# Expert gate and up products from high and low halves, in a one-core transformer layer with attention and a mixture of experts

## Chip, cores and metric

One core of a Trainium2 chip runs the whole layer in one launch. The metric is the device time of that launch in microseconds (us), as the median of several executions; lower is better. Durations of single instructions come from one profiled execution.

## The reference

The input is B, N, HID = 4, 512, 256 in float32, so 2048 tokens. The layer has two halves, each followed by a residual and a layer norm:

```python
x = layernorm(x + attention(x)); x = layernorm(x + ffn(x))
# attention: H = 16 query heads, KV = 4 key heads, D = 128
q, k, v = x @ Wq, x @ Wk, x @ Wv
y   = softmax(causal(rope(q) @ rope(k).T / sqrt(D))) @ v
S_t = S_(t-1) * exp(log_sigmoid(k_t) / 16) + softmax(k)_t v_t^T;  o_t = softmax(q)_t @ S_t
attention = (0.5 * y + 0.5 * o) @ Wo
# ffn: E = 8 experts, F = 176, each token takes its 2 likeliest
p = softmax(x @ gate_w.T); w, e = top_k(p, 2)
ffn = sum over the 2 experts e: w * ((silu(x @ w_gate[e]) * (x @ w_up[e])) @ w_down[e])
```

## The kernel before

**Engines.** Each engine has an instruction stream written out by hand: PE (TensorE), ACT (ScalarE), DVE (VectorE), POOL (GpSimd), SP (which issues DMAs). Instructions of a stream run in order, and the streams meet at semaphores (`wait_ge`, `then_inc`). Nothing reorders them.

**Attention part.** The work is 16 groups g (4 batches by 4 key heads) of C = 4 chunks c of 128 tokens, 64 steps. `step(g, c)` exists once for each engine. PE's order in a step is score, gla_matrix, gate_sums, project (of the chunk two ahead), output (the product with Wo of the step before), turn_weights (transposes of the softmax weights), turn (transposes of the next chunk's queries and decayed features `qd`, then of keys at L523, which waits for this step's add_output), gather (the products with V). The products of projection, scores and output use high and low halves: each f32 operand is split into two f32r tiles, hi (a copy on ACT) and lo (the difference, on POOL or DVE), and hi x hi, hi x lo, lo x hi are summed. POOL's order in a step is weigh_features, move_v, decay (L1500 is its second half; it gives `qd`), rotate, then x_split, split of a staged weight, norm1 and send. DVE adds the output product to the token rows `acc` in add_output (L1064), near the middle of its step.

**Routing.** In the last eight groups, counted as steps k = 0 to 31, the first three batches (set 0, 12 tiles of 128 tokens) are routed beside attention. Tables give the step of each piece and whether DVE does it in the middle ("mid") of its step, before add_output, or at the end ("late"): COMPARE_AT, RANK_AT, EXP_AT, COUNT_AT, BASES_AT, SLOTS_AT. Then `send(t)` (L1566) on POOL writes each token's row twice, by indirect DMA, into the slots of its two experts in DRAM (`slot_x`), two DMAs for a tile, by SEND_AT. Before that SP has cleared the slots. GU_IN and DN_IN give the steps in which SP loads expert weights over the projection weights of key heads that are done.

**Expert loop.** The slots of set 0 make NT_A = 31 tiles, those of the fourth batch (set 1) NT_B = 15; NT = 46. For q = 1 to 47 PE does turn_x(q+1) (L677), gate_up(q) (L689), down(q-2) (L706), turn_h(q-1). ACT does h_out(q-2), x_out(q+1), silu(q) (L908), y_out(q-2) (L917), and its norm2 of finished tokens in q = 42 and 43 and behind the loop. DVE does multiply(q) (L1336) and way_back(q). `gate_up` waits for x_out's copy. In the first iterations DVE and PE also route set 1, and in iterations 14 to 17 POOL sends its four tiles. POOL's `send_back(q)` (L1573) writes a finished tile's rows by indirect DMA into `plane`, from one of YO = 5 buffers `yo`. SP loads slots three tiles ahead (L417), and from q = 38 rows of `plane`, which DVE combines from iteration 37 on (combine, moments2 or shift2 in turn). moments2 and shift2 of a batch use four columns `mv`, `ve`, `rstd`, `nmr` that all batches share, so moments2 waits for norm2 of the batch before.

**The end.** After y_out(45) the last write goes out, SP loads the rows of the last four tiles, DVE combines them, POOL's rs2 gives 1/deviation, ACT normalises, SP stores.

Of the kernel before, what the change touches and what calls it, by code (L numbers as in the profile page):

```python
# [84 lines left out]
def layer_kernel(nc, x_rows, x_cols, wqkv, wo_in, wgu, wdn, gate, rope_cos, rope_sin, cmat, cmask, slot_x, plane, out):  # L85
    with ExitStack() as ctx:
# [10 lines left out]
        with nc.sbuf_tensor("w_hi", [P128, KV * KT2 * QKV], F32R) as w_hi, \  # L97
                nc.sbuf_tensor("w_lo", [P128, KV * KT2 * QKV], F32R) as w_lo:
            pass
        gu_w = sb("gu_w", [P128, E, GUW], F32)  # L100
        spare = sb("spare", [P128, KV * KT2 * QKV - E * GUW], F32)
        dn_w = sb("dn_w", [P128, E, DNW], F32)
        spare2 = sb("spare2", [P128, KV * KT2 * QKV - E * DNW], F32)
        wo_hi = sb("wo_hi", [P128, H * HID], F32R)
        wo_lo = sb("wo_lo", [P128, H * HID], F32R)
# [60 lines left out]
        mv = [None] + [sb(f"mv{i}", [P128, 4, 2], F32) for i in (1, 2)]  # L166
        ve = [None] + [sb(f"ve{i}", [P128, 4], F32) for i in (1, 2)]
        rstd = [None] + [sb(f"rstd{i}", [P128, 4], F32) for i in (1, 2)]
# [27 lines left out]
        nmr = sb("nmr", [P128, TPB], F32)  # L196
# [9 lines left out]
        xT = rqT[:, :].rearrange("p (a n) -> p a n", a=2)  # L206
# [50 lines left out]
        s_zf, s_guw, s_dnw = (sem(n) for n in ("s_zf", "s_guw", "s_dnw"))  # L257
# [5 lines left out]
        s_mark, s_back, s_bf = sem("s_mark"), sem("s_back"), sem("s_bf")  # L263
        s_yg = [sem(f"s_yg{i}") for i in range(4)]
# [10 lines left out]
        wo_jobs = [(wo_in[:, a:b], wo_hi[:, a:b], wo_lo[:, a:b]) for a, b in  # L275
                   ((a, min(a + WJOB, H * HID)) for a in range(H * HID // 2, H * HID, WJOB))]
        jobs = proj_jobs(1) + proj_jobs(2) + wo_jobs[0:2] + proj_jobs(3) + wo_jobs[2:]
        n_attn = len(jobs)

        def jobs_of(g, c):  # L280

            u = C * g + c
            return () if u == 1 else (0, 1) if u == 0 else (u,) if u < n_attn else ()
# [7 lines left out]
        COMPARE_AT = {("late", 9): 0, ("late", 13): 1, ("mid", 21): 2}  # L291
# [3 lines left out]
        SLOTS_AT = {("mid", 24): 0, ("mid", 25): 1}  # L295
        SEND_AT = {25: (0, 2), 26: (2, 4), 27: (4, 6), 28: (6, 8), 29: (8, 10), 30: (10, 12)}
# [9 lines left out]
        GU_IN = {18: (0, 2), 22: (2, 4), 26: (4, 6), 30: (6, 8)}  # L306
        DN_IN = {18: (0, 3), 22: (3, 6), 26: (6, 8)}
# [55 lines left out]
        def _(sp):  # L363
# [31 lines left out]
            def load_experts(k):  # L395
                for e in range(*GU_IN.get(k, (0, 0))):
                    sp.wait_ge(s_proj, C * (NG - KV + last_kv(e, GUW) + 1))
                    sp.dma_start(gu_w[:, e, :], wgu[:, e, :]).then_inc(s_guw, 16)
                for e in range(*DN_IN.get(k, (0, 0))):
                    sp.wait_ge(s_proj, C * (NG - KV + last_kv(e, DNW) + 1))  # L400
                    sp.dma_start(dn_w[:, e, :], wdn[:, e, :]).then_inc(s_dnw, 16)
# [40 lines left out]
            for t in range(NT - 38, TILES):  # L442
                load_rows(t)
            ov = out.rearrange("b (t p) n -> p (b t) n", p=P128)
            for n in range(3):
                sp.wait_ge(s_xo, TPB * (n + 1))
                sp.dma_start(ov[:, TPB * n:TPB * (n + 1), :], acc[:, TPB * n:TPB * (n + 1), BODY]).then_inc(s_out, 16)
# [1232 lines left out]
```

## Time and profile before

| | |
|---|---|
| median of 3 runs | 981.12 us (980.0 to 983.92) |
| the profiled execution | 980.99 us |
| its span, first instruction to last | 979.2 us |
| busy: PE, DVE, ACT, POOL | 928.0, 654.4, 661.8, 636.1 us |
| TensorE's granted clock, mean | 0.98 of full |

A busy time says how long an engine had an instruction running; a wait in brackets behind a row says how long the engine stood before it, and what released it. The granted clock is given as a share of 2.4 GHz, 0.50 is 1.2 GHz.

### The profile page before, as it was taken

How to read it: one execution, taken by the hardware profiler on the slowest of the kernel's cores; microseconds unless marked ns; L12 is line 12 of the kernel's file. 1: busy time of each engine (PE TensorE's matmuls, PEld its weight loads, DVE VectorE, ACT ScalarE, POOL GpSimd, SP SyncE). 2: the span in 40 equal slices, each digit the busy share in tenths (PEclk: the TensorE clock that was granted, in tenths of full speed). 3: DMA queues.
4: the chain of work that ended last, by engine and by line, in shares of the span. 5: the costliest groups of instructions: out<-in, count | busy, mean ns of one | idle time of the engine just before them, and what ended most of it. 6: DMA issues, size and time to landing. Idle time of an engine off the chain costs nothing.

```text
span 979.2 us, 18417 instructions
## 1 busy us (share of the span) xinstructions
PE 928.0 (95%) x5347; PEld 718.5 (73%) x5347; DVE 654.4 (67%) x1597; ACT 661.8 (68%) x2139; POOL 636.1 (65%) x609
## 2 busy tenths in 40 slices
PE   7899999999999999999999999999999989989990
PEld 4678777778787878787887877878777766766770
DVE  4777776767676767677676869676887664431274
ACT  6677777777777777777677776777667664543453
POOL 6878675767565657676767667766658881553342
PEclk9999999999999999999999999999999999997995
DMA  7101100000000000900000000010102121332364
GB/s 250 34 17 33 39 1 2 6 12 6 1 0 0 0 1 10 257 6 2 1 1 1 1 7 6 24 39 3 61 1 79 38 85 45 92 107 84 98 180 133
DMA packets 34050, 43.20 MB, mean 44 GB/s; under 512 B 3756, under 2 KB 27950, under 8 KB 33840
## 3 DMA queue, kind: packets, MB, share of 16 engines
q1 hardware_dynamic: 30224, 33.76, 11.8%
q0 software_dynamic: 3744, 8.43, 2.4%
q8 instruction: 41, 0.67, 0.3%
q14 instruction: 41, 0.34, 0.1%
HBM read 25.58 MB, written 18.43 MB: 45 GB/s over the span
## 4 chain that ended last, share of the span: by engine, by line
PE 85%; DVE 4%; ACT 4%; issue 3%; POOL 2%; another core or an unknown queue 1%; DMA 0%; POOLq 0%; DVEq 0%; ACTq 0%
PE OA L590 14%; PE PR L473 12%; PE S L543 11%; PE MS L563 9%; PE S L572 7%; PE S L689 5%; PE OA L552 5%; PE OA L583 4%; PE OA L706 4%; PE PR L519 3%; PE PR L513 3%; PE S L534 1%; PE MS L502 1%; ACT eqk L821 1%; PE MS L594 1%
## 5 line engine op out<-in xcount | busy, mean ns | idle before, releaser
L1496 POOL TENSOR_TENSOR qd<-eqk,eg 128x512 f32<-128x512 f32 x63 | 75.9, 1205 | 163.1 <-issue 157.2
L590 PE MATMUL OA<-wT,V 128*128 128x512 f32 x320 | 150.2, 600 | 0.2 <-DVE wT L1081 0.2
L783 ACT ACTIVATE S<-S,nm 128x128 f32<-128x128 f32 (+3 forms) x256 | 126.8, 495 | 26.8 <-DVE nm L998 22.8
L821 ACT ACTIVATE eqk<-qkv,nmx 128x128 f32<-128x128 f32 x320 | 124.4, 396 | 6.0 <-DVE nmx L1073 5.5
L998 DVE TENSOR_REDUCE nm<-S 128x2 f32<-128x256 f32 (+3 forms) x128 | 102.0, 817 | 29.1 <-PE S L543 23.4
L590 PEld LDWEIGHTS OA<-wT,V 128*128 128x128 f32 x320 | 60.2, 192 | 70.9 <-issue 70.4
L1484 POOL TENSOR_TENSOR eqk<-eqk,rse 128x640 f32<-128x640 f32 x63 | 79.7, 1265 | 49.9 <-DVE rse L1116 25.7
L1032 DVE TENSOR_TENSOR pr<-S,rl 128x256 f32<-128x256 f32 (+3 forms) x128 | 105.5, 824 | 5.0
L1473 POOL TENSOR_TENSOR rp<-qkv,cos 128x640 f32<-128x640 f32 x64 | 99.9, 1560 | 6.4 <-ACT qkv L811 4.9
L1476 POOL TENSOR_TENSOR rp<-rp,rt 128x640 f32<-128x640 f32 x64 | 99.5, 1554 | 5.0
L1473 POOL TENSOR_TENSOR rt<-qkv,sin 128x640 f32<-128x640 f32 x64 | 99.5, 1555 | 0.0
L842 ACT COPY wT<-S 128x512 f32<-128x512 f32 x96 | 51.6, 591 | 51.7 <-PE S L572 51.7
L1573 POOL DMA_INDIRECT plane<-eqk,back x46 | 45.5, 989 | 61.7 <-ACT eqk L917 52.9
L572 PE MATMUL S<-cm,pr 128*128 128x128 f32 x640 | 80.4, 273 | 3.5 <-DVE pr L1032 3.5
L563 PE MATMUL MS<-wo_hi,oT_hi 128*128 128x256 f32 (+1 forms) x256 | 76.0, 297 | 3.5 <-DVE gc L1041 2.9
L473 PE MATMUL PR<-w_hi,ring_hi 128*128 128x512 f32 (+1 forms) x252 | 74.7, 377 | 1.0 <-ACT qkv L811 1.0
L572 PEld LDWEIGHTS S<-cm,pr 128*128 128x128 f32 x640 | 71.2, 141 | 4.3 <-DVE pr L1032 2.7
L563 PE MATMUL MS<-wo_hi,oT_lo 128*128 128x256 f32 (+1 forms) x256 | 72.2, 282 | 0.0
L563 PE MATMUL MS<-wo_lo,oT_hi 128*128 128x256 f32 (+1 forms) x256 | 72.1, 282 | 0.0
L473 PE MATMUL PR<-w_hi,ring_lo 128*128 128x512 f32 (+1 forms) x252 | 71.1, 363 | 0.0
L543 PE MATMUL S<-KT_hi,rq_hi 128*128 128x256 f32 (+2 forms) x192 | 68.8, 359 | 0.0
L552 PE MATMUL OA<-qdT,kdT 128*128 128x512 f32 x128 | 65.6, 594 | 1.5 <-DVE oT_lo L990 1.5
(173 smaller groups left out, 2506.1 us busy)
## 6 DMA issues: line engine op xcount, KB each, us to landing
qkv<-slot_x SPq DMA_DIRECT2D x46, 129.0 KB
pr<-plane SPq DMA_DIRECT2D x16, 256.0 KB, 3.1
gu_w<-in_wgu SPq DMA_DIRECT2D x8, 352.0 KB, 3.6
slot_x<-zero SPq DMA_DIRECT2D x2, 1290.0 KB, 9.8
stage<-in_wqkv SPq DMA_DIRECT2D x6, 384.0 KB, 3.4
xraw<-in_x_cols SPq DMA_DIRECT2D x16, 128.0 KB, 2.4
acc<-in_x_rows SPq DMA_DIRECT2D x1, 2048.0 KB, 11.1
dn_w<-in_wdn SPq DMA_DIRECT2D x8, 256.0 KB, 4.2
```

The lines of the kernel that those rows point to most:

```text
L473: last = pe.matmul(PR[:, a:b], x[:, cc, k, :], wq_cols(w, kv, k, a, b), start=(i == 0), stop=(i == len(steps) - 1))
L543: last = pe.matmul(S[:, h, 0:n], q[:, h * 128:(h + 1) * 128], k[:, 0:n], start=False, stop=(i == len(steps) - 1), skip_group_check=True)
L552: pe.matmul(OA[:, :], kdT[:, :], qdT[:, c % 2, :], start=True, stop=True).then_inc(s_at, 1)
L563: last = pe.matmul(MS[:, 0:HID], o[:, h * 128:(h + 1) * 128], r, start=(i == 0), stop=(i == len(steps) - 1))
L572: last = pe.transpose(S[:, j, h * 128:(h + 1) * 128], pr[:, h, j * 128:(j + 1) * 128], ident)
L590: last = pe.matmul(OA[:, :], V[:, j, :], wT[:, j, :], start=(c == 0 and j == 0), stop=(j == c))
L783: nc.scalar.activation(S[:, h, 0:n], S[:, h, 0:n], ACT.Exp, bias=nm[:, h:h + 1], scale=1.0, accum_out=ls[:, h:h + 1]).then_inc(s_exp, 1)
L821: last = nc.scalar.activation(eqk[:, par, h * 128:(h + 1) * 128], qkv[:, c % C, h * 128:(h + 1) * 128], ACT.Exp, bias=nmx[:, h:h + 1], sca ...
L998: nc.vector.tensor_reduce(nm[:, 2 * pair:2 * pair + 2], S[:, 2 * pair:2 * pair + 2, 0:n], AX_X, ALU.max, negate=True).then_inc(s_nm, 1)
L1032: nc.vector.tensor_tensor(pr[:, h, 0:n], S[:, h, 0:n], rl[:, h].rearrange("p (h o) -> p h o", o=1) .to_broadcast([P128, 2, n]), ALU.mult). ...
L1473: nc.gpsimd.tensor_tensor(to.rearrange("p (h w d) -> p h w d", w=2, d=64), src, tab, ALU.mult).then_inc(s_rt, 1)
L1476: nc.gpsimd.tensor_tensor(rp[:, c % 2, :], rp[:, c % 2, :], rt[:, :], ALU.add).then_inc(s_rp, 1)
```

## The change

- The expert weights of gate and up are kept as `gu_hi` and `gu_lo` (f32r). They pass through `stage` like the attention weights: SP loads (GU_IN, four steps or fewer ahead), ACT copies the high half at the head of its step, POOL subtracts at the end of its step (SPLIT_AT). `dn_w` comes in one DMA in step 26, over the Wo halves of key heads that are done; `wo` therefore holds both halves, interleaved by key head, and its jobs are 512 columns wide.
- `gate_up` is six f32r products instead of two of f32. x_out writes `xT_hi`, and a new DVE instruction `x_low` writes `xT_lo`; it stands first in DVE's iteration.
- POOL does norm1 and send ahead of split. SEND_AT leaves step 28 out and puts three tiles in step 30 and one in step 31. In the expert loop the eight row writes of set 1 go one in each of the iterations 15 to 22, where two went in each of 14 to 17.
- compare(2) goes from the middle of step 21 to the end of 20, slots from the middle of 24 and 25 to the ends of 23 and 24, and tile_experts(0) from slot_bases (step 23) to the end of 26.
- `mv`, `ve`, `rstd`, `nmr` of the second norm have a column for each of the 16 tiles, and moments2's wait for `s_xo` is gone. combine starts one iteration sooner; norm2 goes one tile in each iteration from q = 40. The last tile is normalised on DVE and stored alone.

The diff, cut to its core:

```diff
-        gu_w = sb("gu_w", [P128, E, GUW], F32)
+        gu_hi = sb("gu_hi", [P128, E, GUW], F32R)
...
+        gu_lo = sb("gu_lo", [P128, E, GUW], F32R)
...
-        wo_hi = sb("wo_hi", [P128, H * HID], F32R)
-        wo_lo = sb("wo_lo", [P128, H * HID], F32R)
...
-        mv = [None] + [sb(f"mv{i}", [P128, 4, 2], F32) for i in (1, 2)]
+        mv = [None] + [sb(f"mv{i}", [P128, (0, 4, TILES)[i], 2], F32) for i in (1, 2)]
...
-        nmr = sb("nmr", [P128, TPB], F32)
+        nmr = sb("nmr", [P128, TILES], F32)
...
-        xT = rqT[:, :].rearrange("p (a n) -> p a n", a=2)
+        xT_hi = rq_hi[:, :].rearrange("p (a n) -> p a n", a=2)
+        xT_lo = rq_lo[:, :].rearrange("p (a n) -> p a n", a=2)
...
+        jobs += [(wgu[:, e, :], gu_hi[:, e, :], gu_lo[:, e, :]) for e in range(E)]
+        SPLIT_AT = {18: 0, 19: 1, 22: 2, 23: 3, 26: 4, 27: 5, 30: 6, 31: 7}
...
-        COMPARE_AT = {("late", 9): 0, ("late", 13): 1, ("mid", 21): 2}
+        COMPARE_AT = {("late", 9): 0, ("late", 13): 1, ("late", 20): 2}
...
-        SLOTS_AT = {("mid", 24): 0, ("mid", 25): 1}
-        SEND_AT = {25: (0, 2), 26: (2, 4), 27: (4, 6), 28: (6, 8), 29: (8, 10), 30: (10, 12)}
+        SLOTS_AT, EXPERTS_AT = {("late", 23): 0, ("late", 24): 1}, ("late", 26)
+        SEND_AT = {25: (0, 2), 26: (2, 4), 27: (4, 6), 29: (6, 8), 30: (8, 11), 31: (11, 12)}
...
-        GU_IN = {18: (0, 2), 22: (2, 4), 26: (4, 6), 30: (6, 8)}
-        DN_IN = {18: (0, 3), 22: (3, 6), 26: (6, 8)}
+        GU_IN = {16: (0, 2), 20: (2, 4), 24: (4, 6), 28: (6, 8)}
+        DN_IN = 26
...
-                if q >= 38:
-                    load_rows(q - 38)
+                if q >= 37:
+                    load_rows(q - 37)
...
-            for t in range(3 * TPB, TILES, 2):
-                sp.wait_ge(s_xo, t + 2)
-                sp.dma_start(ov[:, t:t + 2, :], acc[:, t:t + 2, BODY]).then_inc(s_out, 16)
-            sp.wait_ge(s_out, 16 * 5)
+            for a, b in ((TPB, 2 * TPB), (2 * TPB, 3 * TPB), (3 * TPB, 3 * TPB + 2), (3 * TPB + 2, TILES - 1)):
+                sp.wait_ge(s_xo, b)
+                store(a, b)
+            sp.wait_ge(s_last, 1)
+            store(TILES - 1, TILES)
+            sp.wait_ge(s_out, 16 * 6)
...
-                pe.wait_ge(s_xT, q + 1)
-                for k in range(KT2):
-                    last = pe.matmul(S[:, q % 2, 0:2 * F], xT[:, q % 2, k * 128:(k + 1) * 128],
-                                     expert_cols(gu_w, expert[q], k * 2 * F, (k + 1) * 2 * F), start=(k == 0), stop=(k == KT2 - 1))
+                pe.wait_ge(s_xl, q + 1)
+                steps = [(k, x, w) for k in range(KT2) for x, w in ((xT_hi, gu_hi), (xT_hi, gu_lo), (xT_lo, gu_hi))]
+                for i, (k, x, w) in enumerate(steps):
+                    last = pe.matmul(S[:, q % 2, 0:2 * F], x[:, q % 2, k * 128:(k + 1) * 128],
+                                     expert_cols(w, expert[q], k * 2 * F, (k + 1) * 2 * F), start=(i == 0), stop=(i == len(steps) - 1))
...
-                if q in (42, 43):
-                    for i in ((0, 1) if q % 4 == 2 else (2, 3)):
-                        norm2(0, i)
+                if q >= 40:
+                    norm2(q - 40)
...
+                if not n1:
+                    x_low(0)
+                    x_low(1)
                 add_gla(g, c)
...
+            def x_low(q):
+                dve.wait_ge(s_xT, q + 1)
+                nc.vector.tensor_tensor(xT_lo[:, q % 2, :], PR[:, (q % 2) * 512:(q % 2) * 512 + 256],
+                                        xT_hi[:, q % 2, :].bitcast(F32), ALU.subtract).then_inc(s_xl, 1)
...
-                later(dve, s_xo, TPB * n - 2 + 2 * h)
...
-            later_tiles = {37 + t: t for t in range(3 * TPB)}
+            later_tiles = {36 + t: t for t in range(3 * TPB)}
             for q in range(1, NT + 2):
+                if q + 1 < NT:
+                    x_low(q + 1)
...
+            nc.vector.tensor_scalar(a, a, mv[2][:, TILES - 1, 0:1], rstd[2][:, TILES - 1:TILES], ALU.subtract, ALU.mult).then_inc(s_last, 1)
...
-                if isinstance(g, int):
-                    for j in jobs_of(g, c):
-                        split(j)
                 if k in STATS_AT:
                     norm1(STATS_AT[k])
                 if k in SEND_AT:
                     for t in range(*SEND_AT[k]):
-                        send(t)
+                        for r in range(2):
+                            send(t, r)
+                if isinstance(g, int):
+                    for j in jobs_of(g, c):
+                        split(j)
...
-            sends = {14: 12, 15: 13, 16: 14, 17: 15}
-            deviations = {36 + 2 * i: (i // 2, i % 2) for i in range(5)}
+            sends = {15 + i: (3 * TPB + i // 2, i % 2) for i in range(2 * TPB)}
+            deviations = {35 + 2 * i: (i // 2, i % 2) for i in range(5)}
```

## Rows read from the trace of the kernel before

**Rows 1.** The page, part 1: engine, busy us, share of the span, instructions.

```profile
PE 928.0 (95%) x5347; PEld 718.5 (73%) x5347; DVE 654.4 (67%) x1597; ACT 661.8 (68%) x2139; POOL 636.1 (65%) x609
```

**Rows 2.** Timeline, 874 to 897: start, us, engine, line, operation, [wait before it <-releaser].

```profile
875.19 1.35 PE L689 MATMUL S<-gu_w,rqT 128*128 x4
...
886.75 0.32 ACT L908 ACTIVATE qd<-S 128x176 f32<-128x176 f32 x1 [3.84 <-remote]
...
891.67 2.55 PE L689 MATMUL S<-gu_w,rqT 128*128 x4
...
895.67 1.35 PE L689 MATMUL S<-gu_w,rqT 128*128 x4
```

**Rows 3.** Timeline of one undisturbed tile's TensorE work.

```profile
940.42 1.35 PE L689 MATMUL S<-gu_w,rqT 128*128 x4
...
941.60 1.03 PE L706 MATMUL OA<-dn_w,am 128*128 x4
...
942.90 1.35 PE L689 MATMUL S<-gu_w,rqT 128*128 x4
```

**Rows 4.** Windows: length, busy us (x count) of five engines, clock, DMA share, GB/s.

```profile
792.30:795.70 3.40, 3.40 (x7) 1.32 (x6) 1.47 (x5) 3.31 (x14) 3.32 (x3) 0.50 0.00 0
881.10:894.70 13.60, 11.02 (x26) 7.47 (x27) 1.33 (x7) 3.89 (x12) 5.82 (x6) 0.50 0.27 91
```

**Rows 5.** Timeline of POOL, row writes of set 1: the first and the last of eight.

```profile
872.40 0.97 POOL L1566 DMA_INDIRECT slot_x<-acc,sloti  x1 [0.30 <-issue]
...
885.14 0.96 POOL L1566 DMA_INDIRECT slot_x<-acc,sloti  x1 [0.30 <-issue]
```

**Rows 6.** Timeline of PE, the first three of an output product's 12 matmuls.

```profile
712.62 0.37 PE L563 MATMUL MS<-wo_hi,oT_hi 128*128 128x256 f32 x1
712.82 0.28 PE L563 MATMUL MS<-wo_lo,oT_hi 128*128 128x256 f32 x1
712.94 0.28 PE L563 MATMUL MS<-wo_hi,oT_lo 128*128 128x256 f32 x1
```

**Rows 7.** Groups by line and shape: out<-in, xcount, busy us, mean ns, idle before.

```profile
L1108 DVE TENSOR_TENSOR rq_lo<-PR,rq_hi 128x512 fp32r<-128x512 f32 x48 | 32.6, 679 | 0.0
...
L1524 POOL TENSOR_TENSOR w_lo<-stage,w_hi 128x768 fp32r<-128x768 f32 x6 | 10.9, 1833 | 0.0
```

**Rows 8.** Timeline of DVE: two multiplies of neighbouring tiles, moments2 between.

```profile
939.67 0.34 DVE L1336 TENSOR_TENSOR rp<-qd,S 128x176 f32<-128x176 f32 x1 [0.39 <-ACT qd L908]
...
942.15 0.34 DVE L1336 TENSOR_TENSOR rp<-qd,S 128x176 f32<-128x176 f32 x1
```

**Rows 9.** Timeline, end of the expert loop: y_out and send_back of tile 45.

```profile
957.16 0.37 ACT L917 COPY eqk<-OA 128x256 f32<-128x256 f32 x1 [1.30 <-PE OA L706]
...
960.23 1.04 POOL L1573 DMA_INDIRECT plane<-eqk,back  x1 [0.19 <-issue]
```

**Rows 10.** Timeline around decay of steps 28 and 29.

```profile
778.32 0.45 POOL L1500 TENSOR_TENSOR qd<-eqk,eg 128x128 f32<-128x128 f32 x1
...
779.42 0.60 PE L519 MATMUL PR<-cm,qd 128*128 128x128 f32 x4
...
791.58 0.66 PE L519 MATMUL PR<-cm,qd 128*128 128x128 f32 x4 [2.08 <-POOL qd L1500]
```

**Rows 11.** Timeline, step 31: last row write of set 0, first slots, turn_x, turn_weights.

```profile
808.38 0.96 POOL L1566 DMA_INDIRECT slot_x<-acc,sloti  x1 [0.30 <-issue]
...
812.18 1.75 SPq L417 DMA_DIRECT2D qkv<-slot_x  x4
...
815.15 0.60 PE L677 MATMUL PR<-cm,qkv 128*128 128x128 f32 x4
...
817.60 0.66 PE L572 MATMUL S<-cm,pr 128*128 128x128 f32 x4 [1.85 <-DVE pr L1032]
```

**Rows 12.** Timeline of PE, turn's key transpose behind a late add_output, steps 21 and 25.

```profile
688.93 0.30 PE L523 MATMUL MS<-cm,rp 128*128 128x128 f32 x1 [1.73 <-DVE acc L1064]
...
740.93 0.30 PE L523 MATMUL MS<-cm,rp 128*128 128x128 f32 x1 [1.18 <-DVE acc L1064]
```

More of the change, by code:

```diff
@@ L396, in load_experts @@
                 for e in range(*GU_IN.get(k, (0, 0))):
[L397 to L401, printed above, removed]
+                    load_job(n_attn + e)
+                if k == DN_IN:
+                    sp.wait_ge(s_op, C * (NG - 2))
+                    sp.dma_start(dn_w[:, :, :], wdn).then_inc(s_dnw, 16)
             def clear_slots(s, a, b):
@@ L439, in _, with store @@
                 load_slots(q)
-                if q >= 38:
-                    load_rows(q - 38)
-            for t in range(NT - 38, TILES):
-                load_rows(t)
[L444 to L447, printed above, removed]
-            for t in range(3 * TPB, TILES, 2):
-                sp.wait_ge(s_xo, t + 2)
-                sp.dma_start(ov[:, t:t + 2, :], acc[:, t:t + 2, BODY]).then_inc(s_out, 16)
-            sp.wait_ge(s_out, 16 * 5)
+                if q >= 37:
+                    load_rows(q - 37)
+            ov = out.rearrange("b (t p) n -> p (b t) n", p=P128)
+            def store(a, b):
+                sp.dma_start(ov[:, a:b, :], acc[:, a:b, BODY]).then_inc(s_out, 16)
+            for t in range(NT - 37, TILES):
+                if t == 3 * TPB:
+                    sp.wait_ge(s_xo, TPB)
+                    store(0, TPB)
+                load_rows(t)
+            for a, b in ((TPB, 2 * TPB), (2 * TPB, 3 * TPB), (3 * TPB, 3 * TPB + 2), (3 * TPB + 2, TILES - 1)):
[4 more added lines that the diff above has]
+            sp.wait_ge(s_out, 16 * 6)
         @block.tensor
@@ L558, in output @@
                 pe.wait_ge(s_oTl, u + 1)
-                steps = [(h, o, w) for h in range(GQ) for o, w in ((oT_hi, wo_hi), (oT_hi, wo_lo), (oT_lo, wo_hi))]
-                for i, (h, o, w) in enumerate(steps):
-                    a = (kv * GQ + h) * HID
-                    r = w[:, a:a + HID] if isinstance(a, int) else w[:, bass.ds(a, HID)]
+                steps = [(h, o, s) for h in range(GQ) for o, s in ((oT_hi, 0), (oT_hi, 1), (oT_lo, 0))]
+                for i, (h, o, s) in enumerate(steps):
+                    a = kv * 2 * GQ * HID + (s * GQ + h) * HID
+                    r = wo[:, a:a + HID] if isinstance(a, int) else wo[:, bass.ds(a, HID)]
                     last = pe.matmul(MS[:, 0:HID], o[:, h * 128:(h + 1) * 128], r, start=(i == 0), stop=(i == len(steps) - 1))
@@ L973, in _ @@
                     router_exp(3)
-                if q in (42, 43):
-                    for i in ((0, 1) if q % 4 == 2 else (2, 3)):
-                        norm2(0, i)
-            for n in (1, 2, 3):
-                for i in range(TPB):
-                    norm2(n, i)
+                if q >= 40:
+                    norm2(q - 40)
+            for t in range(NT + 2 - 40, TILES - 1):
+                norm2(t)
         @block.vector
@@ L1449, in _ @@
                         shift2((t - 2) // TPB, ((t - 2) % TPB) // 2)
-            combine(3 * TPB - 1)
-            moments2(2, 1)
             shift2(2, 1)
@@ L1555, in norm1, with send @@
                                         ALU.subtract, ALU.mult).then_inc(s_x1a, 1)
-            def send(t):
+            def send(t, r):
                 s = 0 if t < SETS[0][1] else 1
-                if t == SETS[s][0]:
+                if t == SETS[s][0] and r == 0:
                     pool.wait_ge(s_sl, s + 1)
@@ L1613, in _ @@
                 if q in sends:
-                    send(sends[q])
+                    send(*sends[q])
                 if q in deviations:
```

63 lines of the change are left out of this document (37 added, 26 removed).

## The prediction

> **What bounds the kernel now.** I read the page first, for busy time. TensorE (PE) is busy in 95% of the span [rows 1], so the question at each place is whether PE is kept waiting and how long its own instructions are. Then I read the chain of waits and the timeline of the expert loop. Between tile 19 and tile 23 the loop takes 20.48 us for four tiles where it needs 4 x 2.48 [rows 2, 3]: 10.5 us are lost. ScalarE (ACT) waits there for results of PE whose release the profile cannot name: the longest of these waits is 3.84 us before the silu at 886.75 [rows 2]. In the same stretch PE's granted clock is 0.50, its lower level of 1.2 GHz, for 13.6 us, after PE had run empty [rows 4]. No other stretch of the loop shows such a wait. What lies on it and nowhere else in the loop are the eight row writes of set 1 (send, L1566), two after each write of a finished tile, issued from 872.40 to 885.14 [rows 5].
>
> In an undisturbed tile, gate_up takes from 940.42 to 941.60, 1.18 us, of the period of 2.48 us, and no engine is waited for [rows 3].
>
> **Gate and up products.** The two f32 products of a tile become six of f32r over 352 columns. The output product is such a group: its first starts 0.20 us before its second where f32 matmuls precede it, and the others follow each other by 0.12 us at 256 columns [rows 6]. Scaled by the columns, 0.12 x 352/256 = 0.165, and the entry costs 0.08 more. So the group takes 0.08 + 6 x 0.165 = 1.07 us: 0.11 less a tile. The Trainium skill, page TensorE: Matmul & The Clock Gate, section Back-to-back issue gap, gives columns/2.4 + 2.5 ns at full clock; by it 352 columns would take 149 ns and 256 take 109. The row shows 120 ns, so the measurement decides. The bounds from rows: no gain at all, if the pitch is 0.183 and not 0.165 (it need not go by the columns alone), and 0.885 us if an f32r product takes half of an f32 record (1.18/4/2 = 0.147), 0.30 less a tile. I take 1.07, the nearest row.
>
> Each tile also gets x_low on VectorE (DVE): 256 columns out of PSUM, an estimate of 0.35 us from the 679 ns for 512 columns [rows 7]. It stands first in DVE's iteration, ahead of multiply, and waits for ACT's x_out, which is done one period before gate_up wants it. In tiles 1 to 35 DVE has room, PE stays the bound, and 36 tiles x 0.11 = **-4.0 us**. In tiles 36 to 44 DVE also combines output rows. An iteration with moments2 fills DVE from multiply at 939.67 to multiply at 942.15 with 2.5 us [rows 8]; with x_low it is 2.8, and one with shift2 about 2.4, so 2.6 on average against 2.37 of PE. DVE becomes the bound, and the saving is lost. In addition norm2 now stands after every y_out from tile 40 on, and the loop down, y_out, norm2, h_out sets the last two short iterations. I put tiles 36 to 47 at **+1.5 us** (bounds 0 and +4, all twelve stretched by 0.35).
>
> **Splitting the expert weights.** Eight low halves go to POOL's steps 18, 19, 22, 23, 26, 27, 30, 31. One of 768 columns took 1.83 us [rows 7], so 704 take 1.7. In steps 18 to 26 POOL has idle time before its next decay, so nothing. The high halves on ACT, 0.8 us each by an estimate (half of POOL's 1.7), stand ahead of exps and delay the normalised weights where PE has little room: **+0.5 us** in all, bounds 0 and 8 x 0.8.
>
> **Row writes of set 0.** Before, step 28 holds four, and decay of step 29 comes late: PE waits 2.08 us for qd and then runs 3.4 us at the lower clock [rows 4, 10], which loses 1.7 more: 3.8. The change puts none in step 28. But step 27 now ends with four writes and a split. Its 1.7 us push decay in step 28, which ended at 778.77 for transposes that began at 779.42 [rows 10]: 0.65 us of room, 1.1 us of new wait. Together **-2.7 us**.
>
> Steps 30 and 31 get three tiles and one, and a split in each. Before, step 30 held four writes, the last issued at 808.38; the slots were asked for when it had landed, at 812.18, 3.8 us later; PE turned them at 815.15 and then waited for DVE until 817.60, 1.85 us idle [rows 11]. Now the last write has four more ahead or beside it (4 x 1.27; eleven DMAs lie from the first to the last issue of [rows 5]) and a split (1.7), with a copy and gaps 7.4 us; POOL gets there 1.6 us sooner, because step 29 no longer starts late. So it is issued 5.8 us later by POOL's time, while PE comes 2.3 us sooner. turn_x stands ahead of turn_weights in PE's queue, and behind turn_weights stand gather, the last output product and the first gate_up. The slots come 5.8 + 2.3 - 0.95 = 7.1 us late, of which the 1.85 us are covered: 5.3 us. (0.95 is the room before: of the 2.97 us from 812.18 to 815.15 I give the load 2.0.) PE is then empty for over 6 us, longer than the 2.08 us that brought the lower clock before, so I add 2.4 us for work at 1.2 GHz. With 0.3 us for decay in step 30: **+8.0 us**; bounds +1.7 (only the split is late) and +12 (clock low as long as in the second of [rows 4]).
>
> **Routing.** compare(2) and the slots leave the middle of steps 21, 24 and 25, where add_output stands behind them and PE waits 1.73 and 1.18 us for it [rows 12]. At the end of a step they cost what DVE's next score_max is late. compare there meets an idle POOL and is short; I take 0.4 us each for steps 20 and 24, nothing behind the long gathers of 23 and 26. 2.9 - 0.8 = **-2.1 us**; bounds -2.9 and +1.
>
> **Row writes of set 1.** They go from two per tile in four tiles to one per tile in eight. POOL issues one DMA every 1.27 us in both, for 15 us before and 20 us after; that period, 2.54, is above PE's 2.37, but five buffers of yo cover the 8 x 0.17 = 1.4 us of lag. If the wait of unknown release comes from two such writes beside a write of a finished tile, it goes: **-10.5 us**. If it comes from the number of writes or from POOL's unbroken issuing, it stays. For going: the output writes alone follow one another without it, and 24 row writes in pairs in the attention part cost PE only what is told above, with nothing else on the queue. I take that it goes, and keep zero as the other bound.
>
> **The tail.** Before, rs2 stands ahead of the last send_back and waits for moments2, which waits for ACT's norm2, for they share four statistics columns. y_out ended at 957.53 and the last write was issued at 960.23 [rows 9]. With own columns it is issued some 0.8 us after y_out: -1.9 us, and every later step, from the last row loads on, moves with it. The last tile's normalisation on DVE saves a hop, but its store is issued behind another: -0.1. **-2.0 us**. If the last write were hidden, nothing would come of it; DVE waits for those rows, so it is not.
>
> The one large load of dn_w and the loads through stage come 4 steps ahead of their use and stand only in SP's queue: nothing.
>
> **Sum**: -4.0 + 1.5 + 0.5 - 2.7 + 8.0 - 2.1 - 10.5 - 2.0 = -11.3 us. The profiled execution took 980.99 us, of which the span is 979.2; the median of the runs is 981.12. 981.0 - 11.3 = **969.7 us**.
>
> **Rivals.**
> *The unnamed wait stays.* Without its term the sum is -0.8: 980.2 us. For it: POOL's queue is as full as before, for longer. Against: the writes are thinned. Chance 0.30. With half of it, 975 us, 0.10.
> *The slots are not late*, because the row writes land sooner or PE has other work: 8 us less, 962 us. Against it speaks that turn_x is in PE's order. Chance 0.05.
> *f32r at full pitch*, as the page named above has it: by rows 0.885 instead of 1.07 a tile, 36 x 0.185 = 6.7 us less, 963 us. The measured 0.12 speaks against it. Chance 0.03.
> *Slower: the clock stays low after the late slots.* At the lower level a tile takes about twice its period; tile 22 to 23 took 4.0 us in [rows 2]. From the forecast, 11.3 us of gain are used up after 11.3/1.63 = 7 tiles at the low clock, and over 0.5% slower is reached after 10, which gives 986 us. For it: 13.6 us of low clock in [rows 4]. Against: it came back there as soon as PE was fed, and the loop feeds PE fully. Chance 0.07.
> The forecast itself has 0.45, with its own range 965 to 975.
>
> **Chances.** 0.5%, 4.9 us, is about what a measurement of this kernel can tell from no change. Faster: 0.45 + 0.05 + 0.03 + most of the half case = 0.62. Same: the wait that stays, 0.30. Slower: 0.08. The range takes in the wait that stays: 963 to 982.
>
> **What would show it.** In the trace after: L689's successor group in 1.07 us and a period near 2.37 us from tile 24 to 35; near 2.6 from 36 on with DVE never idle; no wait of unknown release around the set 1 writes and clock 1.0 there; a PE idle of 5 us or more ahead of turn_weights in step 31, with the lower clock behind it; step 29 near 11.5 us; the last send_back within 1 us of y_out. The prediction is wrong if the unnamed wait is still there or has moved, or if the slots arrive in time.

## The result and the profile after

The changed kernel took 973.62 us (median of 5 runs, 973.2 to 974.16) against 980.12 us for the kernel before beside it (5 runs, 977.59 to 983.92). The ratio is 0.9928, 95% interval 0.9907 to 0.995: 0.7% faster, 6.5 us by the medians. The forecast was 969.7 us, 11.3 us faster, with a range of 963 to 982 and 965 to 975 for the likeliest case. The profiled execution took 973.68 us with a span of 971.9 us.

Where the two spans (979.2 and 971.9 us) differ, by the start of each stage in the two traces (differences are of the unrounded times):

| stage | before | after | difference |
|---|---|---|---|
| start to PE's step 31 | 809.8 | 810.0 | +0.2 |
| step 31 to gate_up of tile 0 | 13.9 | 18.3 | +4.4 |
| gate_up(0) to y_out(45) | 133.5 | 123.4 | -10.0 |
| y_out(45) to the end | 22.0 | 20.1 | -1.9 |

The page of the kernel after, part 1:

```profile
PE 919.2 (95%) x5439; PEld 728.8 (75%) x5439; DVE 671.8 (69%) x1644; ACT 666.6 (69%) x2147; POOL 649.4 (67%) x618
```

PE stays busy for 95% of the span, as in [rows 1].

**One tile.** The timeline of the kernel after, PE only, for one tile of the loop:

```profile
871.86 0.27 PE L717 MATMUL S<-cm,rp 128*128 128x128 f32 x1
871.97 0.38 PE L695 MATMUL PR<-cm,qkv 128*128 128x128 f32 x2
872.11 0.40 PE L708 MATMUL S<-gu_hi,rq_hi 128*128 x1
872.35 0.32 PE L708 MATMUL S<-gu_lo,rq_hi 128*128 x1
872.51 0.32 PE L708 MATMUL S<-gu_hi,rq_lo 128*128 x1
...
873.15 1.02 PE L725 MATMUL OA<-dn_w,am 128*128 x4
...
874.37 0.41 PE L708 MATMUL S<-gu_hi,rq_hi 128*128 x1
```

The six f32r products of gate_up (L708) follow each other by 0.16 us, and the group lasts from 872.11 to 873.15, 1.04 us against 1.18 in [rows 3]. The period is 2.26 us against 2.48: 0.22 less a tile, twice what I forecast. The rest is at the other end. gate_up now starts 0.14 us after turn_x (L695 to L708); in the trace before, that step took 0.22.

**From tile 36 on.** DVE's multiplies of four neighbouring tiles in the kernel after:

```profile
931.50 0.33 DVE L1358 TENSOR_TENSOR rp<-qd,S 128x176 f32<-128x176 f32 x1
...
934.25 0.33 DVE L1358 TENSOR_TENSOR rp<-qd,S 128x176 f32<-128x176 f32 x1
934.48 0.42 PE L708 MATMUL S<-gu_hi,rq_hi 128*128 x1 [0.22 <-DVE rq_lo L1362]
...
936.59 0.33 DVE L1358 TENSOR_TENSOR rp<-qd,S 128x176 f32<-128x176 f32 x1
...
939.38 0.33 DVE L1358 TENSOR_TENSOR rp<-qd,S 128x176 f32<-128x176 f32 x1
```

An iteration with moments2 takes 2.75 and 2.79 us, one with shift2 2.34, and PE waits for x_low (L1362, the bracket at 934.48). That is the change of bound which the prediction named, with its sizes (2.8 and 2.4).

**Set 0's slots.** The timeline of the kernel after, PE's three longest waits from step 28 on, with POOL's last writes and SP's first slot loads:

```profile
781.00 0.66 PE L537 MATMUL PR<-cm,qd 128*128 128x128 f32 x4 [1.82 <-POOL qd L1528]
...
800.86 0.51 PE L581 MATMUL MS<-wo,oT_hi 128*128 128x256 f32 x2 [2.59 <-issue]
...
810.04 0.96 POOL L1594 DMA_INDIRECT slot_x<-acc,sloti  x1 [0.30 <-issue]
811.03 1.71 POOL L1552 TENSOR_TENSOR gu_lo<-stage,gu_hi 128x704 fp32r<-128x704 f32 x1
...
814.44 0.97 POOL L1594 DMA_INDIRECT slot_x<-acc,sloti  x1 [0.30 <-issue]
...
816.95 1.75 SPq L429 DMA_DIRECT2D qkv<-slot_x  x4
...
819.27 1.08 PE L695 MATMUL PR<-cm,qkv 128*128 128x128 f32 x4 [3.74 <-DMA qkv<-slot_x]
```

Windows of the kernel after; the clock is the third number from the end:

```profile
801.00:805.00 4.00, 4.00 (x22) 4.00 (x23) 1.30 (x2) 0.94 (x3) 3.53 (x6) 0.57 0.10 33
820.00:825.00 5.00, 5.00 (x20) 4.23 (x19) 1.54 (x3) 2.46 (x5) 0.00 (x0) 0.50 0.03 12
868.00:904.00 36.00, 30.12 (x177) 26.54 (x177) 16.30 (x71) 15.55 (x51) 19.98 (x21) 1.00 0.37 112
```

The last write of set 0 is issued at 814.44, 6.1 us later than in [rows 11]; the slots are asked for 4.8 us later and turn_x starts 4.1 us later, after a wait of 3.74 us, and 5 us at 1.2 GHz follow. Step 28's decay is late as forecast (1.82 us of waiting, 1.1 forecast). Step 30 has a longer wait in front of the output product than before (2.59 us; 1.71 before), and 4 us at a clock of 0.57.

**Tiles 16 to 23.** The third window shows what the largest term was about. PE is busy for 30.12 of 36 us, so it still stands there, now at full clock. The periods between y_outs are 3.08, 4.51, 1.94, 2.25, 5.50, 1.95, 2.74 and 3.86 us for tiles 17 to 24. From tile 14 to 29 the loop takes 41.3 us where 15 x 2.26 = 33.9 would do: 7.4 us lost, against 47.8 - 15 x 2.49 = 10.4 before. ACT in this stretch of the kernel after:

```profile
881.02 0.37 ACT L925 CAST rq_hi<-PR 128x256 fp32r<-128x256 f32 x1 [0.81 <-remote]
883.86 0.32 ACT L929 ACTIVATE qd<-S 128x176 f32<-128x176 f32 x1 [2.47 <-PE S L708]
884.07 0.37 ACT L938 COPY eqk<-OA 128x256 f32<-128x256 f32 x1
884.32 0.39 ACT L933 COPY am<-S 128x256 f32<-128x256 f32 x1
884.59 0.41 ACT L925 CAST rq_hi<-PR 128x256 fp32r<-128x256 f32 x1
884.85 0.36 ACT L929 ACTIVATE qd<-S 128x176 f32<-128x176 f32 x1
```

Five instructions that wait for five different groups of PE (gate_up, down, turn_h, turn_x, gate_up again) start one right behind the other. PE had begun those groups at 878.89, 880.34, 881.30, 881.52 and 881.99. ACT runs in order, so the rows alone show only that the first release was late. The trace also keeps semaphore updates, though not all. The records of the five groups end at 880.09, 881.47, 881.69, 881.90 and 883.21, and the updates of their semaphores stand at 883.83, 883.89, 883.94, 883.98 and 884.05. So the first release comes 3.7 us after its group's record has ended, and five of them come within 0.22 us. The kernel before has the same: the silu at 886.75 [rows 2] waits for a gate_up whose record ends at 879.02, and the update stands at 886.72, 7.7 us later.

**The tail.** The kernel after, last y_out, last row write, first combine behind it:

```profile
951.73 0.37 ACT L938 COPY eqk<-OA 128x256 f32<-128x256 f32 x1 [1.30 <-PE OA L725]
...
952.87 0.97 POOL L1601 DMA_INDIRECT plane<-eqk,back  x1 [1.38 <-ACT eqk L938]
...
957.79 0.48 DVE L1380 SCALAR_TENSOR_TENSOR acc<-pr,wts,acc 128x256 f32<-128x256 f32 x1 [3.01 <-DMA pr<-plane]
```

The last write is issued 1.14 us after y_out begins, 3.07 in [rows 9].

### The profile page after: what moved, and what is told of

Read it like the earlier page. It is cut to its first block, busy times and chain, and to the rows that moved or that the text cites. A ratio compares the mean times of both kernels' runs of the same rounds, so it can differ in the third digit from the quotient of the medians.

```text
span 971.9 us, 18753 instructions
## 1 busy us (share of the span) xinstructions
PE 919.2 (95%) x5439; PEld 728.8 (75%) x5439; DVE 671.8 (69%) x1644; ACT 666.6 (69%) x2147; POOL 649.4 (67%) x618
## 4 chain that ended last, share of the span: by engine, by line
PE 79%; DVE 6%; ACT 6%; issue 3%; POOL 2%; DMA 2%; another core or an unknown queue 0%; SPq 0%; DVEq 0%; POOLq 0%; ACTq 0%
PE OA L608 12%; PE PR L491 12%; PE S L561 10%; PE MS L581 9%; PE S L590 7%; PE OA L570 5%; PE S L708 4%; PE OA L601 4%; PE OA L725 3%; PE PR L531 3%; PE PR L537 3%; ACT eqk L842 2%; POOL slot_x L1594 1%; PE MS L520 1%; PE S L552 1%
## 5 line engine op out<-in xcount | busy, mean ns | idle before, releaser
L1017 DVE TENSOR_REDUCE nm<-S 128x2 f32<-128x256 f32 (+3 forms) x128 | 101.8, 817 | 28.6 <-PE S L561 24.4
L581 PE MATMUL MS<-wo,oT_hi 128*128 128x256 f32 (+1 forms) x512 | 99.0, 291 | 5.9 <-issue 2.6
L581 PEld LDWEIGHTS MS<-wo,oT_hi 128*128 128x128 f32 x512 | 79.4, 191 | 14.3 <-DVE gc L1060 8.3
L590 PE MATMUL S<-cm,pr 128*128 128x128 f32 x640 | 83.1, 278 | 2.9 <-DVE pr L1051 2.9
L590 PEld LDWEIGHTS S<-cm,pr 128*128 128x128 f32 x640 | 73.6, 144 | 4.1 <-DVE gc L1060 2.5
L581 PE MATMUL MS<-wo,oT_lo 128*128 128x256 f32 (+1 forms) x256 | 72.6, 284 | 0.0
```

What stands on the lines that cost most here:

```text
L581: last = pe.matmul(MS[:, 0:HID], o[:, h * 128:(h + 1) * 128], r, start=(i == 0), stop=(i == len(steps) - 1))
L590: last = pe.transpose(S[:, j, h * 128:(h + 1) * 128], pr[:, h, j * 128:(j + 1) * 128], ident)
L1017: nc.vector.tensor_reduce(nm[:, 2 * pair:2 * pair + 2], S[:, 2 * pair:2 * pair + 2, 0:n], AX_X, ALU.max, negate=True).then_inc(s_nm, 1)
```

## Experiments

The variants ran in four groups, each group on another chip. The kernel before, run beside each group, took 970.6, 970.2, 978.5 and 969.7 us, and 980.1 in the first measurement. Times are compared only within a group. Where a sentence sets traces of different groups side by side, it says so.

### What the row writes of set 1 are worth

The first group has four variants of the changed kernel. `pairs_again`:

```diff
-            sends = {15 + i: (3 * TPB + i // 2, i % 2) for i in range(2 * TPB)}
+            sends = {14: 12, 15: 13, 16: 14, 17: 15}
...
-                    send(*sends[q])
+                    send(sends[q], 0)
+                    send(sends[q], 1)
```

> The changed kernel with only the row writes of set 1 back in pairs, iterations 14 to 17. If thinning them is what took the lost time around tile 20 from 10.5 to 7.4 us, this takes 3 us longer than the changed kernel (977 us) with a low clock after the wait. If the pairs don't matter, it is within 1 us of 973.6.

`no_set1_writes` takes these lines away, and SP's wait for `s_sent[1]`; `set1_rows_dropped` keeps the instructions and drops their rows. Both leave set 1 out of the result and clear its part of `plane` beforehand.

```diff
-                nc.gpsimd.indirect_dma_start(slot_x[s], bass.IndirectOffsetOnAxis(ap=sloti[:, r, t:t + 1], axis=0),
-                                             acc[:, t, :], None).then_inc(s_sent[s], 16)
+                to = bass.IndirectOffsetOnAxis(ap=sloti[:, r, t:t + 1], axis=0)
+                if s:
+                    nc.gpsimd.indirect_dma_start(slot_x[s], to, acc[:, t, :], None, bounds_check=0, oob_is_err=False).then_inc(s_sent[s], 16)
...
```

> Leaves out the eight row writes of set 1 (its tiles are then all padding, and 1 MB of plane is cleared ahead of the routed steps so that its rows are defined). If the late release of ACT by PE comes from these writes, tiles 19 to 27 run at a period of 2.26 us and the time is 7 us lower, 966 us. If the lateness belongs to something else at that place, it stays and the time is within 1.5 us of 973.6.

> The same eight instructions on POOL at the same places, but with a bound of 0 on the slot number, so that POOL issues each and next to no row is written (set 1 is left out of the result, plane is cleared as in the run without writes). If POOL's unbroken issuing makes the late releases, they stay and the time is 972 to 974 us. If the rows on their way to DRAM make them, they go and it is about 966 us, as without the writes.

Measured, with the kernel before at 970.61 us: pairs_again 965.88 us (ratio 0.9948, 0.9932 to 0.9965), no_set1_writes 966.22 (0.9949, 0.9933 to 0.9966), set1_rows_dropped 965.82 (0.9949, 0.9932 to 0.9965). All three are equal, and no trace of them shows a lost microsecond in tiles 15 to 35. So the 966 us without the writes, which the expectation gave as the sign that the writes make the lateness, does not show it: the pairs have 966 us too. To see whether that came from the variants or from the chip, both kernels were run unchanged in the next group.

> The kernel before, unchanged, for its profile beside the others. On the chip of the runs above, the kernel before took 970.6 us, 10 us less than on the chip of the two traces, and four variants of the changed kernel, with set 1's writes in pairs, spread, dropped or left out, all ran tiles 16 to 30 at an even 2.26 us. If the lateness around tile 20 belongs to the chip or its surroundings, the period stays 2.49 us there too in this profile and the span is near 969 us. If it belongs to the kernel before alone, periods of 6 and 7 us stand around tile 18 again.

> The changed kernel, unchanged. If the lateness belongs to the chip, this takes 966 us here, like the run with pairs, with a ratio of 0.995; if the one-by-one writes bring it about, it takes some 7 us more than the run with pairs and is slower than the kernel before.

The kernel before: 969.64 us, and 970.24 in the runs beside it (ratio 0.9991, 0.9982 to 1.0001). The changed kernel: 965.98 us, ratio 0.996 (0.9946 to 0.9974). Windows of the kernel before on this chip:

```profile
868.00:904.00 36.00, 36.00 (x176) 27.71 (x176) 12.41 (x63) 18.03 (x59) 21.71 (x23) 1.00 0.42 127
```

The changed kernel with pairs:

```profile
868.00:904.00 36.00, 36.00 (x225) 33.54 (x224) 19.81 (x83) 19.72 (x64) 23.30 (x24) 1.00 0.46 136
```

PE is busy for 36.00 of 36 us in both, at full clock, with all eight writes in the window. The periods of all tiles from 15 to 35 are 2.49 and 2.26 us. So the lateness that I priced at 10.5 us does not follow from the kernel before: the same instructions on another chip don't have it. Here the change is worth 4.3 us, 0.4%, against 6.5 us in the first measurement.

The third group fell on a chip where the kernel before took 978.48 us. It held two kernels that differ only in the edit of pairs_again (both with the weight splits behind the writes, see below):

> The same kernel as the run with the splits last, but set 1's row writes in pairs in iterations 14 to 17. On a chip without the lateness around tile 20 the two are equal within 0.5 us. On one with it, this is longer by what thinning is worth there: 3 us by the difference of the two first traces (10.5 to 7.4 us lost), 0 if the lateness does not depend on how the writes stand.

Spread 970.86 us (970.19 to 972.19), pairs 971.87 us (970.49 to 973.46). Windows of the spread one:

```profile
868.00:904.00 36.00, 30.01 (x176) 26.39 (x176) 15.44 (x66) 15.27 (x50) 20.37 (x21) 1.00 0.37 113
```

Of the one with pairs:

```profile
868.00:904.00 36.00, 29.64 (x172) 26.92 (x171) 14.98 (x63) 15.19 (x48) 19.57 (x21) 0.95 0.36 109
```

Both lose about 6 us of PE's time in the window. With pairs the loss lies in tiles 16 to 19 (periods 3.15, 8.56, 2.89, 2.97), spread in tiles 17 to 24 (3.14, 4.56, 1.95, 2.26, 5.54, 1.95, 2.70, 3.86). The loss moves with the writes and hardly shrinks: thinning them gives 1.0 us by the medians, whose ranges overlap, and 42.44 - 41.47 = 0.97 us by the stretch from tile 14 to 29 in the two traces. No kernel without these writes ran on such a chip, so that the writes bring the loss about is not shown either. One last run asked whether the rows themselves or POOL's instructions bring it about.

> The run with set 1's rows dropped once more, since the chip of its first run showed no lateness in any kernel. The kernel before, timed beside it, tells whether this chip shows it (978 to 980 us) or not (970). On a chip that does: 965 to 967 us and even periods of 2.26 us if the rows on their way to DRAM make the lateness; 972 to 974 us with uneven periods in tiles 16 to 23 if POOL's issuing of these instructions makes it, or anything else there. On a chip that does not: 966 us, and the question stays open.

965.73 us, with 969.73 for the kernel before: a chip without the lateness, so this stays open.

One more thing sets the chips apart. The five traces with the lateness hold 6766 to 7000 semaphore updates, the nine others 7811 to 7926, and nearly all that is missing lies behind 700 us. Whether the recording has a part in the lateness, or both come from something else on these chips, no run tests.

### What the halves and the rest are worth

`halves_alone` is the changed kernel with the edit of pairs_again and the tables of before:

```diff
-        COMPARE_AT = {("late", 9): 0, ("late", 13): 1, ("late", 20): 2}
+        COMPARE_AT = {("late", 9): 0, ("late", 13): 1, ("mid", 21): 2}
...
-        SLOTS_AT, EXPERTS_AT = {("late", 23): 0, ("late", 24): 1}, ("late", 26)
-        SEND_AT = {25: (0, 2), 26: (2, 4), 27: (4, 6), 29: (6, 8), 30: (8, 11), 31: (11, 12)}
+        SLOTS_AT, EXPERTS_AT = {("mid", 24): 0, ("mid", 25): 1}, ("late", 23)
+        SEND_AT = {25: (0, 2), 26: (2, 4), 27: (4, 6), 28: (6, 8), 29: (8, 10), 30: (10, 12)}
```

> The changed kernel with the routing tables of before (compare in the middle of step 21, slots in the middle of 24 and 25, tile_experts in 23), the row writes of set 0 in steps 25 to 30 and those of set 1 in pairs in iterations 14 to 17. Left of the change: products from halves, weight splits, own statistics columns, later norm2. If the halves are worth what the two traces say (period 2.26 instead of 2.49 us over some 36 tiles, -8.3) and the low halves of the weights stand on the way in steps 26 to 31, this takes between 970 and 977 us, with the ten microseconds of lateness around tile 20 as long as before. If the gain came from the spread writes and the tables, it is within 3 us of the kernel before.

966.15 us in the first group, ratio 0.9949 (0.9932 to 0.9965), against 965.88 for pairs_again. The whole new schedule of routing and row writes gives 0.3 us, which is nothing that can be told. The traces show why. pairs_again reaches step 31 at 808.9, halves_alone at 815.4: 6.5 us earlier. But turn_x(0), behind set 0's slots, starts at 819.9 and 820.8, and gate_up(0) at 828.2 and 828.9. Of the 6.5 us, 2.8 lie in step 30 (16.75 us against 13.94), where the clock was at 0.54 from 804 to 808 in halves_alone and at 1.00 in pairs_again. What is saved in the steps, by the tables or by the clock, is waited for in front of the slots. set1_rows_dropped shows the same with the tables of pairs_again: its step 30 was slow too (16.81 us), it reaches step 31 at 812.0, and gate_up(0) starts at 828.0.

`rest_alone` is the other half: the products in f32, with the weights loaded whole and neither splits nor x_low, everything else kept.

```diff
-                pe.wait_ge(s_xl, q + 1)
-                steps = [(k, x, w) for k in range(KT2) for x, w in ((xT_hi, gu_hi), (xT_hi, gu_lo), (xT_lo, gu_hi))]
+                pe.wait_ge(s_xT, q + 1)
+                steps = [(k, xT_hi, gu_hi) for k in range(KT2)]
```

> The changed kernel with gate and up products in f32 as before (two products, weights loaded whole, no splits, no x_low), and the rest of the change kept: routing tables, row writes, own statistics columns, later norm2. The halves gave 6.9 us between the first gate_up and the last y_out in the traces of one chip and cost some microseconds of late slots; the tail gave 1.9. If that sum holds, this is 1 to 4 us faster than the kernel before. If the tables and writes of the change only help together with the halves, it is within 1 us of it.

974.58 us against 978.48, ratio 0.9956 (0.9941 to 0.9971), on the third group's chip. Its PE reaches step 31 at 806.4, 3.4 us before the kernel before in its first trace, and still has to wait for the slots:

```profile
814.20 0.88 PE L696 MATMUL PR<-cm,qkv 128*128 128x128 f32 x4 [2.36 <-DMA qkv<-slot_x]
```

gate_up(0) starts at 825.2, 1.5 us later than in the first trace of the kernel before and 0.4 later than in before_here, both on other chips. PE waits for the slots without any weight split. The 3.9 us are within the 1 to 4 expected, but the sum behind them is not borne out. The stretch from tile 14 to 29 loses 4.7 us here (42.0 for 37.3) and lost 10.5 in the first trace of the kernel before. That is 5.8 us of lateness, more than the whole gain. So this run does not show that the schedule gains anything but the tail.

### What makes the slots late

`send30` sends the last tile in step 30, ahead of both splits:

```diff
-        SEND_AT = {25: (0, 2), 26: (2, 4), 27: (4, 6), 29: (6, 8), 30: (8, 11), 31: (11, 12)}
+        SEND_AT = {25: (0, 2), 26: (2, 4), 27: (4, 6), 29: (6, 8), 30: (8, 12)}
```

> The changed kernel with the last tile of set 0 sent in step 30 instead of 31, so the two weight splits stand behind all row writes. If the late slots in front of step 31's turn_x (PE waits 3.7 us for them in the first trace of the changed kernel, then runs 5 us at half clock) come from the split between the writes, turn_x starts 2 us sooner and the time falls by 2 to 5 us. If something else is last there, nothing changes.

963.36 us (963.25 to 963.68, the changed kernel beside it 965.98), ratio to the kernel before 0.993 (0.9914 to 0.9946). turn_x of the changed kernel in this group:

```profile
818.99 1.15 PE L695 MATMUL PR<-cm,qkv 128*128 128x128 f32 x4 [5.11 <-DMA qkv<-slot_x]
```

And of send30:

```profile
812.70 0.96 POOL L1594 DMA_INDIRECT slot_x<-acc,sloti  x1 [0.30 <-issue]
...
815.15 1.75 SPq L429 DMA_DIRECT2D qkv<-slot_x  x4
...
817.33 1.15 PE L695 MATMUL PR<-cm,qkv 128*128 128x128 f32 x4 [3.26 <-DMA qkv<-slot_x]
```

turn_x starts 1.7 us sooner, the wait falls from 5.11 to 3.26 us, the clock is back sooner, and gate_up(0) starts at 824.9 and not at 827.5; 2.6 us in all. (The two profiled spans differ by 1.9 us only: send30's last tile takes 3.29 us and not 2.43, with a mean clock of 0.68 from 938 to 943 where after_here has 1.00.) The split stood between the writes and was on the path.

`high_late` moves ACT's copies of the high halves behind copy_out:

```diff
                     for j in jobs_of(g, c):
-                        job_high(j)
+                        if k is None or k < 26:
+                            job_high(j)
                 exps(g, c)
...
+                if k is not None and k >= 26:
+                    for j in jobs_of(g, c):
+                        job_high(j)
                 if not n1:
                     x_out(0)
```

> The changed kernel with ACT's copies of the high halves in steps 26, 27, 30 and 31 moved from ahead of the exponentials to behind copy_out. In step 30 the copy (0.76 us) lengthens PE's wait for gc to 2.59 us against 1.71 before, and the clock falls behind it. If the copy is the cause, step 30 takes 13.0 us and not 15.5, and the time falls by 1 to 3 us; if the clock falls anyhow, step 30 stays at 14 to 15.5 us.

965.66 us against 965.98: nothing, where 1 to 3 us were expected. Its PE:

```profile
800.59 0.50 PE L581 MATMUL MS<-wo,oT_hi 128*128 128x256 f32 x2 [2.12 <-DVE gc L1064]
...
819.21 1.14 PE L695 MATMUL PR<-cm,qkv 128*128 128x128 f32 x4 [5.53 <-DMA qkv<-slot_x]
```

The wait in step 30 falls from 2.59 to 2.12 us, so the copy was part of it. The slow step 30 that it was to cure (15.5 us in the first trace of the changed kernel) was not there on this chip: after_here has the same wait of 2.59 us and a clock of 1.00 from 801 to 805. Step 30 takes 13.5 us and not 13.9, and the wait for the slots grows to 5.53. The copy costs nothing as long as the slots are last.

`splits_last` adds to send30 that steps 26 and 27 hold no split:

```diff
-        SPLIT_AT = {18: 0, 19: 1, 22: 2, 23: 3, 26: 4, 27: 5, 30: 6, 31: 7}
+        SPLIT_AT = {18: (0,), 19: (1,), 22: (2,), 23: (3,), 30: (4, 5), 31: (6, 7)}
```

The loads of jobs 6 and 7 stand behind the first three slot loads, the ACT copies of 4 and 5 behind copy_out, those of 6 and 7 behind weights_out.

> The changed kernel with all of set 0's writes done in step 30, and the splits of experts 4 to 7 behind them (4 and 5 at the end of step 30, 6 and 7 in step 31; their loads behind the first three slot loads, their ACT copies behind the exponentials). Steps 26 and 27 then hold no split on POOL. If the split of 1.7 us in each is what makes step 28's decay late (PE waited 1.8 us for qd, step 28 took 10.8 us and not 8.8), step 28 takes 8.8 to 9.5 us, turn_x comes 2 us sooner than in the run with the last tile in step 30, and the time falls from 963.4 to about 961 us. If gate_up of tile 0 then waits for the splits, it starts as late as before and the time stays.

970.86 us against 978.48, ratio 0.9911 (0.9881 to 0.9941). Step 28 takes 8.79 us and not 10.8, so the split before it was the cause of that wait; rest_alone, without splits, has 8.78. PE then waits for DVE as well:

```profile
812.95 1.23 DVE L1026 TENSOR_REDUCE nm<-S 128x2 f32<-128x1024 f32 x1 [1.63 <-remote]
...
815.15 0.41 PE L697 MATMUL PR<-cm,qkv 128*128 128x128 f32 x2 [2.17 <-DMA qkv<-slot_x]
...
817.48 1.76 PE L592 MATMUL S<-cm,pr 128*128 128x128 f32 x7 [1.26 <-DVE pr L1060]
```

turn_x starts at 815.15, but score_max (L1026) had waited 1.63 us for a release that the profile can't name, as around tile 20 on such chips. turn_weights follows at 817.48 at half clock, and gate_up(0) starts at 826.0, 1.1 us later than send30's. Whether this kernel beats send30 on one chip, as the expected 961 us would have it, was not measured. The nearest statement is by ratios to the kernel before, 0.991 and 0.993 on different chips, and their intervals overlap.

## Why the prediction was right or wrong

The sign held and the time lies in the range, but the gain was 6.5 us and not 11.3 (4.3 on the chip of the second group), and that it came so near is luck: the errors of the terms cancel. By the prediction's own sign, "if the unnamed wait is still there or has moved", its mechanism was wrong, for the wait was still there and had moved (tiles 17 to 24, before 17 to 20). By its own steps, with the first pair of traces and the pair on the chip without the lateness (before_here and after_here, spans 969.9 and 963.7):

| term | forecast | first chip | other chip |
|---|---|---|---|
| products and loop, without tiles 16 to 24's loss | -4.0 + 1.5 | -7.0 | -6.9 |
| row writes of set 1 | -10.5 | -3.0 | 0 |
| up to gate_up(0): splits, set 0's writes, routing | +3.7 | +4.6 | +2.7 |
| tail | -2.0 | -1.9 | -1.9 |
| sum (of the unrounded times) | -11.3 | -7.3 | -6.2 |

**Row writes of set 1: the step that failed.** "I take that it goes" put down 10.5 us to two writes beside a third. On chips without the lateness pairs cost nothing, and on one with it spreading them gave 1.0 us of some 8. I had read a wait from one execution on one chip as a property of the kernel. That the -3.0 us of the first pair come from the spread is not shown: the test of pairs against spread gives 1.0. The loss itself varies: from tile 14 to 29 it is 10.4 us in the kernel before, 7.4 in the one after, 7.6 and 8.5 in the two of the third group, and 4.7 in rest_alone (42.0 - 15 x 2.49), which spreads the writes too but has f32 products. What sets its length stays open; the low clock of [rows 4] is in none of the spread ones. The rival that the wait stays, 0.30 with half of it at 0.10, was nearer in mechanism. It gave 980 and 975 us, and the larger gain of the products made up the difference.

**Gate and up products: mechanism right, size off.** The group was forecast at 1.07 us and took 1.04. But I compared the group alone. The transposes in front of it are f32, and gate_up starts sooner behind them (0.14 for 0.22 us). The term of 36 x 0.11 = 4.0 measured 7.4 us from y_out(0) to y_out(35) in before_here and after_here (91.23 and 83.88), where 36 x 0.22 would be 7.9. The row shows 0.16 us for 352 columns; by the rule that I cited (the Trainium skill, page TensorE: Matmul & The Clock Gate, section Back-to-back issue gap) it would be 0.149. The trace has 7% more, and 10% more at 256 columns in [rows 6]. The same section calls that rule the gap of an isolated product, and says that in a stream where each product has its own weight load both set the spacing. This kernel is such a stream: its page counts as many weight loads as products, 5439.

**DVE from tile 36 on: right.** The ten tiles up to the last y_out take 24.9 us after and 24.4 before, so these tiles are no faster than before and their saving is gone, as forecast (2.6 us a tile forecast, 2.49 measured).

**Set 0's writes and splits: right in net, wrong in two parts.** The last write was to come 5.8 us later and came 6.1 later. The slots were to hold PE for 7.1 us and held it for 3.7, on the other chip for 5.1. PE did not come 2.3 us sooner but 0.4 later, though step 29 saved its 3.9 us (3.8 forecast), because steps 22, 26, 28 and 30 took 1.9, 0.5, 2.0 and 2.5 us more (28's is the wait of 1.8 that was forecast as 1.1), and the slots were asked for 2.5 us after the last write's issue where [rows 11] have 3.8. That 3.8 is itself the exception: the thirteen other traces, before_here among them, have 2.5 to 3.0. Of step 22 (15.13 us for 13.28) I had said nothing: rank stands at the end of step 21, and with compare gone it starts 1.85 us sooner (689.37 for 691.22), beside POOL's rotate, which is busy until 691.8. Two of its DVE instructions take 1.05 and 1.66 us there; each took 0.42 before, with POOL idle from 691.4. In before_here POOL's rotate ends at 692.6, the second takes 1.66 there too, and step 22 has 14.50 us.

The 3.8 us of step 29 were a reading of one execution as well. The kernel before on the other chip, the wait and the clock behind it:

```profile
792.35 0.66 PE L519 MATMUL PR<-cm,qd 128*128 128x128 f32 x4 [2.08 <-POOL qd L1500]
...
792.30:795.70 3.40, 3.35 (x13) 1.92 (x14) 1.40 (x5) 2.66 (x12) 3.32 (x3) 1.00 0.00 0
```

The wait is the same 2.08 us, the clock stays at 1.00 where [rows 4] have 0.50, and step 29 takes 13.8 us and not 15.4. There the change saves 2.2 us in it.

**Routing: right in the steps of the first chip, worth nothing in the end.** Steps 21, 24 and 25 save 1.8, 0.4 and 1.1 us, and PE waits for the slots instead. Of these, step 21 is again one execution's: its compare (L1176) took 1.76 us in the first trace and 0.63 in before_here, where the wait of [rows 12] is nearly gone and the step saves 0.35 us.

```profile
688.46 0.30 PE L523 MATMUL MS<-cm,rp 128*128 128x128 f32 x1 [0.18 <-DVE acc L1064]
```

The forecast booked the steps' saving and the wait for the slots. It did not say that one eats the other: once the slots are last, nothing saved in the attention steps counts.

**Tail: right**, and the same on both chips.

## What to carry to other kernels

Before a stall with no named release is priced as part of a change, it should be seen in a second execution on another chip; here the kernel before had it in one of its two traces, and by its times in two measurements of five, for 8 to 10 us. The same holds for a short wait and for the clock behind it: three more readings of the first trace (3.8 us of landing, 1.7 us of a late add_output, the low clock of step 29) were not there in the second. When a queue's last transfer decides when the next stage starts, savings on the other engines ahead of it were void here, and the first thing to ask of a new instruction is whether it stands ahead of that transfer in its queue: one split of 1.7 us moved behind the last row write gave 2.6 us. When one group of matmuls gets another type, the switch to its neighbours is priced with it.

## What the runs showed of the hardware

- Equal programs differ by 8 to 10 us between chips (969.7, 970.2 and 970.6 us on three, 978.5 and 980.1 in the other two measurements), nearly all of it in one place. There, with row writes by indirect DMA beside a TensorE loop, semaphore updates of TensorE stand up to 3.7 us (kernel after) and 7.7 us (kernel before) behind the end of their groups' records, five of them within 0.22 us. The place moves with the writes; the cause is open.
- One product of f32r follows another by 0.12 us at 256 columns [rows 6] and 0.16 us at 352 (kernel after, from 872.35).
- A wait of 3.74 us of TensorE in front of turn_x was followed by 5 us at 1.2 GHz in the first trace of the changed kernel; 5.11 us in after_here by a mean clock of 0.57 over 8 us, and 3.26 us in send30 by 0.79. A shorter wait does not tell what the clock does: behind 2.08 us in front of step 29's transposes it was 0.50 for 3.4 us in the first trace of the kernel before and 1.00 in before_here, and behind 2.59 us in step 30 it was 0.57 for 4 us in the first trace of the kernel after and 1.00 in after_here.
- Indirect row writes of 128 rows left GpSimd 1.27 us apart, and the slots were asked for 2.5 to 3.0 us after the last one's issue in thirteen of fourteen traces (3.8 in the other).
